# A new order of work for two phases of a decoder kernel, and a merged score product in the third

## The reference, cut to what matters

```python
# layer 0
x = ln(x + causal_attention_16_heads(x, fourier_bias))      # phase 1
x = ln(x + cross_attention_16_heads(x, ctx[64 keys], mask)) # phase 1
x = ln(x + moe_8_experts_top2_plus_2_shared(x))             # phase 2
# layer 1
x = ln(x + causal_attention_16_heads(low_rank_qkv(x)))      # phase 2
# second cross attention, one head of 256                   # phase 3
kh = ctx @ Wk + bk;  vh = kh @ Wv + bv;  qh = x @ Wq + bq
scores = where(mask == 0, -10000, qh @ kh.T)
x = ln(x + (softmax(scores) @ vh) @ Wo + bo)
x = ln(x + relu(quantum(x @ W1 + b1)) @ W2 + b2)            # phase 3
```

## Time and profile before

| | us |
|---|---|
| median of three runs | 3624.59 |
| the three runs | 3622.93, 3624.59, 3631.72 |
| the profiled execution | 3628.03 |
| its span, first to last instruction | 3626.1 |
| busy share of the span | PE 92%, DVE 72%, ACT 63%, POOL 28% |
| phase 1, first store to last | 253.5 to 1302.3 |
| phase 2, first store to last | 1630.5 to 2984.0 |
| phase 3, first store to last | 3147.0 to 3622.3 |

### The profile page before, as it was taken

The page is one execution under the profiler, slowest core; times in us unless marked ns, Lnnn a source line. Parts: engine busy times, 40 slices in busy tenths (PEclk is TensorE's granted clock), DMA queues, the critical chain, the costliest instruction groups (busy, mean ns, idle before and its releaser), DMA issues.

```text
span 3626.1 us, 59862 instructions
## 1 busy us (share of the span) xinstructions
PE 3344.5 (92%) x20706; PEld 2528.1 (70%) x20706; DVE 2625.4 (72%) x7153; ACT 2283.5 (63%) x4067; POOL 1022.4 (28%) x1576
## 2 busy tenths in 40 slices
PE   5999999999999848999999999999999876999998
PEld 4677777777777636777777777777777655766664
DVE  5688888888888644677777777777777534788876
ACT  3677777777777622456666555556556543677776
POOL 2244444444444422222222322222223110000000
PEclk8999999999999979999999999999999877999999
DMA  7654545445544021444444444444444421011010
GB/s 193 101 95 84 88 96 107 84 88 95 107 84 82 17 82 53 84 80 77 86 92 94 94 88 88 90 89 93 92 87 88 73 44 62 12 36 35 25 35 24
DMA packets 203403, 283.27 MB, mean 78 GB/s; under 512 B 48929, under 2 KB 131874, under 8 KB 194274
## 3 DMA queue, kind: packets, MB, share of 16 engines
q1 hardware_dynamic: 203106, 279.46, 38.2%
HBM read 179.49 MB, written 96.73 MB: 76 GB/s over the span
## 4 chain that ended last, share of the span: by engine, by line
PE 71%; ACT 11%; DVE 7%; DMA 5%; issue 4%; SPq 1%; POOL 1%; PEld 0%; POOLq 0%; ACTq 0%; PEldq 0%; DVEq 0%
PE ps L829 35%; PE ps L1003 8%; PE ps L978 7%; PE ps L1201 5%; PE ps L1017 5%; ACT q_stack L1669 5%; PE ps L953 3%; DMA qk_scratch<-parts 3%; ACT pt L1686 2%; PE ps L984 1%; PE ps L1077 1%; PE ps L888 1%; PE ps L1028 1%; DMA k_stack<-qk_scratch 1%; DVE nmax L1351 1%
## 5 line engine op out<-in xcount | busy, mean ns | idle before, releaser
L1686 ACT ACTIVATE pt<-ps 128x512 f32<-128x512 f32 x1280 | 735.9, 598 | 346.7 <-PE ps L1003 338.8
L1889 POOL TENSOR_SCALAR_AFFINE_SELECT pt<-pt 128x256 f32<-128x256 f32 x1024 | 392.1, 419 | 704.9 <-ACT pt L1686 704.9
L978 PE MATMUL ps<-k_stack,q_stack 96*128 96x512 f32 (+3 forms) x2048 | 547.2, 338 | 42.3 <-ACT q_stack L1669 11.8
L1358 DVE CUSTOM_DVE_ANT_0 ps<-ps,future 128x512 f32<-128x512 f32 (+3 forms) x1024 | 481.7, 515 | 141.9 <-PE ps L978 138.8
L1003 PE MATMUL ps<-q_stack,k_stack 100*128 100x512 f32 (+3 forms) x2048 | 538.6, 345 | 29.3 <-ACT q_stack L1669 23.4
L1003 PEld LDWEIGHTS ps<-q_stack,k_stack 100*128 100x128 f32 x2048 | 351.5, 195 | 124.9 <-ACT q_stack L1669 37.2
L978 PEld LDWEIGHTS ps<-k_stack,q_stack 96*128 96x128 f32 x2048 | 355.6, 194 | 103.2 <-ACT q_stack L1669 18.8
L1351 DVE TENSOR_REDUCE nmax<-ps 128x1 f32<-128x512 f32 (+2 forms) x768 | 354.4, 502 | 92.0 <-PE ps L984 91.0
L1895 POOL TENSOR_TENSOR rs<-rs 128x4 f32<-128x4 f32 x96 | 97.1, 1012 | 1062.0 <-DVE rs L1394 1062.0
L1669 ACT ACTIVATE q_stack<-ps 4x512 fp32r<-4x512 f32 x512 | 300.8, 588 | 64.7 <-PE ps L992 56.5
L1017 PE MATMUL ps<-pt,v_ones 128*32 128x512 f32 (+3 forms) x4096 | 312.1, 446 | 5.7 <-POOL pt L1889 5.3
(11 more groups left out here) (278 smaller groups left out, 7958.6 us busy)
## 6 DMA issues: line engine op xcount, KB each, us to landing
qk_scratch<-parts SPq DMA_DIRECT2D x64, 1024.0 KB, 5.5
q_stack<-qk_scratch SPq DMA_DIRECT2D x384, 128.0 KB, 4.9
k_stack<-qk_scratch SPq DMA_DIRECT2D x384, 128.0 KB, 5.6
gate_of<-gate_scratch SPq DMA_DIRECT2D x128, 256.0 KB, 5.6
x_mid<-x_ring SPq DMA_DIRECT2D x32, 512.0 KB, 3.9
x_ring<-x_mid SPq DMA_DIRECT2D x32, 512.0 KB, 5.3
x_ring<-in_x SPq DMA_DIRECT2D x16, 512.0 KB, 3.8
out_dram<-x_ring SPq DMA_DIRECT2D x16, 512.0 KB, 2.9
```

Source lines behind the costliest of these rows:

```text
L978: done = e.matmul(bank(bank_of[piece])[:, at:at + width], a.q[0:96, base + h, t * P:(t + 1) * P], a.k[0:96, base + h, 0:width], start=a.la ...
L1358: done = e.tensor_tensor_reduce(src, src, future[:, SEQ - width:SEQ], -1.0, 3e38, ALU.add, ALU.min, nmax[:, g % 2, to:to + 1])
L1686: e.activation(dst, src, ACT.Exp).then_inc(exp_up.sem)
L1889: done = e.affine_select(out=blk, in_=blk, compare_op=ALU.is_ge, fill=0.0, base=0, pattern=[[0, 2], [1, P]], channel_multiplier=-1)
```

## The change

There are two parts.

**The order.** The offsets of phases 1 and 2 are replaced for every engine, and the periods become 72.744 and 90.623 instead of 70.45 and 91.45. The set of pieces is the same, and so is what each does. Sorted by the offsets, most neighbours keep their places. Those of phase 2 that move and are spoken of below: on SP `send` of the next row's first half and the `sg` of expert 4 stood behind `rows` of group 3 and now stand ahead of it; `rows` of group 2 stood ahead of `sg` of expert 2 and now stands behind it. On DVE the split `h3` of expert 6 stood behind unit `S` 3 of group 3 and now stands ahead of unit 2; similar moves for experts 9, 0 and 2. On PE `tm v1` stood right before two `S` units, two `T` units and `up` of expert 2, and the two `dn` of expert 0 now come between; the second `dn` of expert 8 moves ahead of the first `T` of group 3, both `dn` of expert 9 move ahead of `gt` or `gr`. In phase 1 on PE: `xs` and `xp` units of the cross attention are moved ahead by one to three places (`xs` 2 ahead of the last `T` of group 1; `xs` 5 and `xp` 3 ahead of the first `T` of group 3), on SP `kl` goes ahead of `rows` of group 3. The order of phase 3 is unchanged but for one added piece.

**The second cross attention (phase 3).** The key parts lie side by side (`a_parts`), so that one matmul of 128 columns makes high x high and high x low at once, in two halves of a bank; `cs` has 16 matmuls instead of 24. DVE copies one half and adds the other. The query bias is no longer added for each row: it is folded once, in the prologue, into the mask's offset. The output bias leaves the product `cw` and becomes an addition on POOL, `tb x1`. Buffers `q_bias`, `unseen`, `ones` go, `sx3` and `offset` come.

```diff
 TABLE = {
-    1: (70.45, {
+    1: (72.744, {
...
-    2: (91.45, {
+    2: (90.623, {
         "sync": {
-            "send": [76.442, 95.983],
-            "rows": [97.435, 117.928, 140.108, 160.952],
-            "sg": [-44.627, -44.367, -30.774, -27.299, -12.417, -5.729, 2.455, 17.582],
+            "send": [82.769, 104.563],
+            "rows": [112.457, 134.686, 155.546, 179.135],
+            "sg": [-36.173, -35.738, -26.135, -20.394, -5.291, 0.424, 9.165, 18.599],
...
     3: (31.45, {
         "gpsimd": {
+            "tb x1": [-26.6],
             "ln x1": [-4.648],
...
-        a_h, a_l = (sb(st3, f"a_{part}", [P, CT, keys_all], F32R) for part in "hl")
+        a_parts = sb(st3, "a_parts", [P, CT, BATCH, 2, CTX], F32R)
...
-        LN_BIAS = {"x0": xo_b, "a1": proj_b}
+        LN_BIAS = {"x0": xo_b, "a1": proj_b, "x1": co_b}
...
-                    ops.append((ones[:, :], co_b[:, :]))
...
-                        ops = []
-                        for c in range(CT):
-                            ops += three(ch[:, c, rows], cl[:, c, rows], a_h[:, c, keys], a_l[:, c, keys])
-                        done = product(e, bank(bank_of[piece])[:, t * CTX:(t + 1) * CTX], ops)
+                        both = bank(bank_of[piece])[:, 2 * t * CTX:2 * (t + 1) * CTX]
+                        done = None
+                        for c, part in ((0, ch), (0, cl), (1, cl), (1, ch)):
+                            wide = part is ch
+                            done = e.matmul(both if wide else both[:, 0:CTX], part[:, c, rows],
+                                            a_parts[:, c, b, :, :].rearrange("p a k -> p (a k)") if wide else a_parts[:, c, b, 0, :],
+                                            start=wide and c == 0, stop=wide and c == 1)
...
+                        for n in range(2):
+                            cols = slice(n * 512, n * 512 + 512)
+                            e.wait_ge(bq_up, n + 1)
+                            e.wait_ge(keys_lo, 12)
+                            e.tensor_tensor(tile32[:, n, :], bank(4 + n), seen[:, cols], ALU.mult).then_inc(mine.up())
+                            e.wait_ge(*mine.now)
+                            e.tensor_tensor(offset[:, cols], offset[:, cols], tile32[:, n, :], ALU.add).then_inc(mine.up())
...
-                    e.tensor_tensor(sc3[:, :, :], bank(bank_of[piece])[:, 0:TT * CTX].rearrange("p (t k) -> p t k", t=TT),
-                                    key_row(q_bias), ALU.add).then_inc(cs_add.sem)
+                    halves = bank(bank_of[piece]).rearrange("p (t a k) -> p t a k", t=TT, a=2)
+                    e.tensor_copy(sx3[:, :, :], halves[:, :, 1, :]).then_inc(mine.up())
+                    e.wait_ge(*mine.now)
+                    e.tensor_tensor(sc3[:, :, :], halves[:, :, 0, :], sx3[:, :, :], ALU.add).then_inc(cs_add.sem)
...
-                        for n in range(2):
-                            e.wait_ge(bq_up, n + 1)
-                            e.activation(q_bias[:, n * 512:n * 512 + 512], bank(4 + n), ACT.Copy)
...
-                elif kind == "prologue":
-                    e.memset(ones[:, :], 1.0)
...
-                        e.dma_start(co_b[:, :], dram["co_b"].partition_broadcast(1)).then_inc(mask_in3, 16)
+                        e.dma_start(co_b[:, :], dram["co_b"].partition_broadcast(P)).then_inc(mask_in3, 16)
```

More of the change, by code:

```diff
@@ L129 @@
 TABLE = {
-    1: (70.45, {
-        "tensor": {
[23 rows of a table removed]
+    1: (72.744, {
+        "sync": {
+            "ld 1": [-95.856],
+            "send": [-38.667, -27.297],
+            "rows": [-31.488, -20.023, -7.387, 16.467],
+            "st 1": [189.153],
+            "kl": [80.759],
+        },
+        "tensor": {
[23 rows of a table added]
         },
         "scalar": {
[17 rows of a table removed]
[17 rows of a table added]
         },
         "vector": {
[18 rows of a table removed]
[18 rows of a table added]
         },
         "gpsimd": {
-            "sel": [23.563, 28.974, 39.371, 41.715, 49.988, 54.887, 67.541, 71.053],
-            "ln a0": [87.769],
-            "tb x0": [94.657],
-            "xs": [107.781, 112.815, 118.398, 123.298, 127.202, 132.423, 139.464, 142.048],
-            "xe": [114.355, 115.773, 121.927, 128.346, 130.395, 135.952, 143.192, 145.006],
-            "ln x0": [160.998],
-        },
-        "sync": {
-            "ld 1": [-102.014],
-            "send": [-45.264, -25.935],
-            "rows": [-40.234, -28.772, 7.159, 10.2],
-            "st 1": [173.474],
-            "kl": [81.835],
-        },
-    }),
@@ L211 @@
-    2: (91.45, {
-        "tensor": {
[25 rows of a table removed]
+            "sel": [31.345, 39.067, 49.299, 53.325, 61.779, 66.3, 78.818, 83.511],
+            "ln a0": [101.581],
+            "tb x0": [109.23],
+            "xs": [120.915, 127.465, 133.169, 138.017, 140.636, 146.113, 153.956, 157.65],
+            "xe": [128.455, 130.248, 136.66, 142.695, 143.685, 149.292, 158.64, 160.618],
+            "ln x0": [178.192],
+        },
+    }),
+    2: (90.623, {
+        "sync": {
+            "ld 2": [-78.284],
+            "send": [82.769, 104.563],
+            "rows": [112.457, 134.686, 155.546, 179.135],
+            "st 2": [279.788],
+            "gh": [-38.533],
+            "sg": [-36.173, -35.738, -26.135, -20.394, -5.291, 0.424, 9.165, 18.599],
+        },
+        "tensor": {
[25 rows of a table added]
@@ L294 @@
+            "sel": [152.034, 156.648, 173.145, 180.159, 199.72, 203.91, 218.585, 226.305],
+            "ln a1": [276.346],
+            "h2": [None, None, -27.497, -21.756, -6.653, -2.324, 7.803, 17.237, 24.112, 31.773],
+            "ln ex": [54.749],
         },
@@ L428, in pieces_of @@
         put("tc", "x1", b)
+        put("tb", "x1", b)
         put("cs", b)
@@ L743, in decoder @@
         cq_b, ck_b, cv_b = (sb(st3, f"{n}_cols", [P, CT]) for n in ("cq_b", "ck_b", "cv_b"))
-        co_b, f2_b = sb(st3, "co_b_row", [1, DIM]), sb(st3, "f2_b_cols", [P, CT])
-        ones = sb(st3, "ones", [1, P])
+        co_b, f2_b = sb(st3, "co_b_rows", [P, DIM]), sb(st3, "f2_b_cols", [P, CT])
         wf2 = sb(st3, "w_down", [P, FT, DIM])
         ff_c, fc = sb(st3, "ff_c", [P, 4 * FT]), sb(st3, "fc", [P, 12, FT])
-        a_h, a_l = (sb(st3, f"a_{part}", [P, CT, keys_all], F32R) for part in "hl")
+        a_parts = sb(st3, "a_parts", [P, CT, BATCH, 2, CTX], F32R)
         v_h, v_l = (sb(st3, f"v_{part}", [P, CT, BATCH, 2, CTX], F32R) for part in "hl")
-        q_bias, seen, unseen = (sb(st3, n, [P, keys_all]) for n in ("q_bias", "seen", "unseen"))
+        seen, offset = (sb(st3, n, [P, keys_all]) for n in ("seen", "offset"))
         W3 = Weights(st3, 3)
@@ L761, in decoder @@
         ch, cl = sb(st3, "xh3", [P, CT, SEQ], F32R), sb(st3, "xl3", [P, CT, SEQ], F32R)
-        sc3 = sb(st3, "sc3", [P, TT, CTX])
+        sc3, sx3 = sb(st3, "sc3", [P, TT, CTX]), sb(st3, "sx3", [P, TT, CTX])
         sm3 = sb(st3, "sm3", [P, 3, TT, 1])
@@ L1520, in vector @@
                     e.wait_ge(*mine.now)
-                    e.tensor_tensor(sc3[:, :, :], sc3[:, :, :], key_row(unseen), ALU.add).then_inc(mine.up())
+                    e.tensor_tensor(sc3[:, :, :], sc3[:, :, :], key_row(offset), ALU.add).then_inc(mine.up())
                     e.wait_ge(*mine.now)
@@ L1631, in scalar @@
                                 done.then_inc(keys_hi)
-                            else:
-                                e.activation((k_h3, None, a_h)[q // 4][:, mt, cols], tile32[:, q % 2, :],
+                            elif q // 4 == 0:
+                                e.activation(k_h3[:, mt, cols], tile32[:, q % 2, :], ACT.Copy).then_inc(keys_hi)
+                            else:
+                                e.activation(a_parts[:, mt, n * 8:n * 8 + 8, 0, :],
+                                             tile32[:, q % 2, :].rearrange("p (b k) -> p b k", k=CTX),
                                              ACT.Copy).then_inc(keys_hi)
-                        for n in range(2):
-                            e.wait_ge(bq_up, n + 1)
-                            e.activation(q_bias[:, n * 512:n * 512 + 512], bank(4 + n), ACT.Copy)
                         for at, res in enumerate((sin_c, cos_c)):
```

23 lines of the change are left out of this document (8 added, 15 removed), and 240 rows, old and new, of the table TABLE.

## The result

The changed kernel takes **3726.35 us** (median; 3720.32 to 3732.62), the kernel before beside it 3623.76 us (3622.74 to 3631.72). The ratio is 1.0279, 95% interval 1.0263 to 1.0295: 2.8% slower, where 3551 us were forecast. The profiled execution took 3722.35 us.

A forecast was written before the change was run, and what follows sets the result against it. It took PE to bound the kernel, its waits being what the order can win. From the profiled 3628.03 us, -53 (phase 2), 0 (phase 1) and -21 (phase 3) gave 3554, or 3551 as a median; range 3524 to 3590.

The forecast's parts named there:

- `rows` behind `sg`: Phase 2, SP: `rows` of group 2 queued behind expert 2's gate load costs 0.4 us per period, 0 to 1.9.
- The prediction's last part: Signs to look for, among them: phase 2 above 94 us with new PE waits ended by a store or `rows` DMA.
- part 1a: New order in phase 2: gains 3.9 us per period, 91.7 instead of 95.6, in all 53 us, ends 20 and 70.
- four waits: Phase 2, PE: first `T` of group 2 1.0, `dn` of expert 6 1.1, `up` 0.5, first `T` of group 3 0.4 us.
- 13.5 periods: Stretch where expert and attention work run side by side; phase 2's 3.9 us per period was multiplied by it to 53.
- Part 1b: New order in phase 1: no wait goes, 0 us per period from -0.6 to +0.7, times 14: 0, from -8 to +10.
- `kl`: Phase 1, SP: putting these 20 DMAs ahead of `rows` of group 3 is covered, as those are issued tens of us early.
- rival B: Slower: phase 1's gap between last exponential and PV, with POOL's selects, becomes bare; 4.5 to 6 us per period; chance 0.05.
- Part 2: Phase 3: fewer score matmuls win 0.86 and the bias row 0.65, 1.5 us per batch row; -21 us with the prologue.
- 0.4 early, not late: Phase 3, DVE: the chain lengthened by one operation is covered because PE's scores end 0.86 us earlier; priced at nothing.
- The prologue's 2.8: Prologue: four more DVE operations of 512 columns ahead of the small constants add 2.8 us on the path.
- A: The waits only move, the same resources ending other waits: 1.5 us gained per period in phase 2, 3588 us; chance 0.13.

The follow-up runs named there:

- e4_rows_first: Changed kernel with one swap on SP in phase 2, `rows` of group 2 again ahead of `sg` of expert 2: 3658.44 us, ratio 1.0092.
- e7_before_swap: Kernel before with one swap alone on SP in phase 2, `sg` of expert 2 ahead of `rows` of group 2: 3688.48 us, ratio 1.0168.
- e5_swap_s10: Changed kernel with `rows` of group 2 ahead of `sg` of expert 2, and `S` 1.0 and 1.1 behind `tm v1` on PE: 3642.51 us, ratio 1.0050.
- e9_old1_fixed2: Changed kernel with phase 1's old order and phase 2's two repairs (`rows` ahead of `sg`, `S` 1.0 and 1.1 behind `tm`): 3595.8 us, ratio 0.9923.
- e1_ph3_only: Kernel before with the phase 3 edit alone, phases 1 and 2 in their old orders: 3613.03 us, ratio 0.9965.
- e6_ph1_pv: Changed kernel with phase 1 moves on PE alone, `PV` of group 2 behind `N` 3 and `xs` 2 behind `S` 3.1: 3757.14 us, ratio 1.0358.
- e14_more: Changed kernel with two phase 2 repairs and phase 1 moves of `PV`, `xs`, `O`, `xe` 4 and `lm x0` on PE, DVE, ACT: 3612.27 us, ratio 0.9970.

## Why the prediction was wrong, point by point

**The term that failed: `rows` behind `sg`.** The prediction priced it "0 to 1.9 per period; I take 0.4", from the time that the gate load takes to issue. The 1.9 rests on a misread row: the 3.82 us of the earlier trace rows are two loads of 0.38 us with a wait between them. The 0.4 was right for what it priced: `rows` now go out 0.44 us behind the last `T` instead of 0.08. What it left out is that 256 KB then travel ahead of them: 3.4 us of landing time, bare, because `rows` of this group had only 0.7 us to spare (landing to `S` 2.0). Both numbers were to be had from the trace of before: the six `rows` DMAs, 768 KB, land in 9.0 us, which makes 3.0 us for 256 KB as an estimate, and the time from the landing to `S` is there to read. Measured, the term is 4.6 us per period (e4_rows_first), and 4.8 in the old order (e7_before_swap), some twelve times the price: 3.2 of it is the wait, and the rest comes with PE's clock, which falls to 1.2 GHz behind most of these waits and for which the prediction had no term. The prediction's last part did name this sign, "a store or `rows` DMA there would be the price of `rows` behind `sg`", and so it was found at once.

**The second omission: `S` 1.0.** I looked at which waits go, not at pieces moved up towards their data. `S` 1.0 came nearer to its `rows` by more than the 2.1 us that it had to spare: 1.4 us of the period (e5_swap_s10).

**The gains of part 1a were real.** Named were 3.0 us from four waits and 1.3 from smaller ones. The losses from start to start at `dn` of expert 6, `T` 2.0, `up` of expert 2 and `T` 3.0 fell by 1.15 + 0.69 + 0.55 + 0.45 = 2.8, where 3.0 were named, and `gr` by 0.43. With the two new waits repaired, phase 2 runs at 93.0, 2.6 less than before, where 91.7 was forecast; `S` 0.4 (0.72) and `tm v1` (0.58) are new and left. But "13.5 periods" was mis-sized; by its own bounds, 1534 to 2762 us, it is 12.8. In e9_old1_fixed2 twelve distances win 30 us against e1_ph3_only, the last three lose 4, and the way to the first store is 340.7 us against 329.8, so the filling costs 11 more. From phase 1's last store to phase 2's last the repaired order wins 1679.3 - 1664.8 = 14.5 us instead of 53. The granted clock of that filling is 0.90 against 0.93, 69 us at 1.2 GHz against 46; half of the difference is 12 us, the size of the loss. That the clock causes it isn't shown: it may follow from waits there that I didn't look for.

**Part 1b: 0, between -8 and +10, was +48.5.** The step that failed is "the same work lies before the wait instead of inside it, and the wait gets longer by what the other got shorter", with "I find no wait that goes": `PV` 0 to 2 and `T` 3.0 lose 4.0 us more and the units `S` only 2.0 less, the wait of `PV` 1 alone went from 0.03 to 1.76 us, and that the moved pieces are short doesn't bound the loss. The 14 periods left out that phase 1 also empties more slowly (13 us in the last three distances, cause open). `kl` was judged rightly: `rows` of group 3 still land 25.5 us ahead of `S` 3.0 (33.5 before). `PV` behind the select was named, as rival B, with 0.05. B's mechanism came: `PV` 0 to 2 lose 3.4 us instead of 0.7, released by POOL. Its size, "4.5 to 6", is about twice what `PV` adds. (Where B evens out the gains, at 5.3 per period, the time would be 3551 + 74 = 3625, not 3632.) That PE's order isn't all of it is shown by e6_ph1_pv: with `PV` and `xs` moved back on PE alone the kernel got slower. The moves on PE, DVE and ACT of e14_more gave back 1.5 of the 2.6 us; where the other 1.1 lies stays open. The chance on slower was far too small because only this one mechanism was allowed to end there.

**Part 2 came nearest.** 24 matmuls became 16 and 2.59 us became 1.74, as forecast. From the changed kernel's timeline, PE:

```profile
3302.26 0.22 PE L1163 MATMUL ps<-a_parts,xh 128*128 128x128 f32 x1
...
3304.00 0.64 PE L1203 MATMUL ps<-act,w_down 128*128 128x512 f32 x1
...
3310.01 0.40 PE L830 MATMUL ps<-yl,w_hi 128*128 128x512 f32 x1
3310.51 1.09 PE L1140 MATMUL ps<-ident,back 128*128 128x128 f32 x8
```

1.74 / 16 = 0.109 us each on average, with half of them 128 columns wide, where it was 0.108 with 64 columns throughout. The Trainium skill's 107 ns for a weight load ("TensorE: Matmul & The Clock Gate", section LDWEIGHTS) stood beside the row's 0.108 in the prediction and is borne out. Its figure for the issue gap is for a matmul by itself; by that nothing would have been won here, and the trace doesn't go by it. `cw` with its bias row fell from 1.42 to 0.71, 0.71 won for 0.65. Together 1.6 per row, but the period fell by only 1.2. Most of the rest shows at `bk`: 3310.51 is 0.50 behind the last matmul start, where 0.23 is the rule in this stretch. DVE's chain behind the scores grew from 2.26 to 2.72 us. I had it "0.4 early, not late" and priced it at nothing; 0.27 of the missing 0.4 stands at `bk` (that the chain causes it is argued from the durations, not tested). And the gain doesn't come 16 times: twelve distances win 1.2 each, 14.4 us, and the last three (29.0, 26.9 and 23.8 us) are the same in both kernels. That makes -14.5 instead of -24. The prologue's 2.8 was 1.9 to 2.3.

**The rivals.** A ("the waits only move") comes near to what happened in phase 2 but stopped at 3588, since it let new waits at most eat the gain. The forecast's range, from 3524 to 3590, excluded every case in which a new wait outgrows the old ones.

## What to carry to other kernels

Price a DMA that is put ahead of another on the same queue by its transfer and not by its issue, and hold this against the time that the later one had to spare. For a new order, list for every moved piece how long its inputs had been ready before: a piece that moves up by more than that adds a wait. Price a wait of PE of some 3 us above its length, since here the clock fell behind it. With engines that work their lists in order, a repair may have to be made on all engines of a chain at once: here a move on PE alone cost 31 us more, and with DVE's and ACT's part of it won 8.

## What the runs showed of the hardware

A load of 256 KB, the 512 gates of one expert spread over 128 partitions, delayed the six DMAs issued right behind it on SP's queue by 3.4 us, a quarter of it by 0.9 us. That is some 75 KB per us, for a load that is cheap in the list of issues because nobody waits for it.

Behind a wait of PE of 3.0 to 3.45 us the granted clock fell to 1.2 GHz for 3.4 or 6.8 us in eight of ten periods of the changed kernel, at some 1.7 us of time for each 3.4; in two periods with the same wait it stayed at 2.4 GHz. Without that wait (e5_swap_s10, e9_old1_fixed2, the kernel before) it stayed up in all ten. Shorter waits had it at times: 1.6 us in e4_rows_first (two periods of ten) and 1.3 us in phase 1 of e6_ph1_pv (five of eight).
